# A Mamba-2 block and a selective scan over 16 images: token halves on 128 partitions, step length with B and C, decays one unit ahead

## The chip, the cores and the metric
One NeuronCore of a Trainium2 chip runs one program. The metric is the device time of an execution in microseconds, the median of the runs. Five engines work side by side: TensorE (PE), VectorE (DVE), ScalarE (ACT), GpSimd (POOL) and SyncE (SP), which issues all transfers of this kernel. They are held in step by semaphores, and each runs its own instructions in the order in which they are written.

## The reference
The input has 16 images of 192 channels and 32x32 = 1024 tokens. Two residual blocks follow each other, all in float32:
```python
x = x + L0(group_norm(x))      # Mamba-2 ("SSD"): 384 inner channels, 12 heads of 32, state 32
x = x + L1(group_norm(x))      # selective scan: 192 channels, state 16

# L0, by token
z, xBC, dt = split(u @ in_proj.T)          # 384, 384+32+32, 12
dt = softplus(dt + dt_bias)
x, B, C = split(silu(depthwise_conv3x3(xBC)))
y = chunked_scan(x, dt, -exp(A_log), B, C, chunk=128) + D * x
out = (layer_norm(y) * norm_w + norm_b) * z @ out_proj.T

# L1, by token
x, delta, B, C = split(seq @ W_proj.T + b_proj)   # 192, 192, 16, 16
delta = softplus(delta + dt_bias)
h = exp(delta * A) * h + (delta * x) * B          # (192, 16) states
out = (sum_n(h * C) + x * D) @ W_out.T + b_out
```

## The kernel before, in words
Channels lie on partitions and tokens along the free dimension. 192 channels are 128 and 64, so each image has an "a" tensor on 128 partitions and a "b" tensor (`xb`, `x1b`, `xnb`) on 64, both with 1024 columns.

The passes form a pipeline over images. In pass b the second block's scans of image b run, and between them the whole first block of image b+1, and the last products of image b-1. A pass has 48 slots; on every engine the code of slot s stands ahead of that of slot s+1. Slot by slot:

- **Scans.** The 192x16 states are 24 units of 128 rows (32 channels by 4 states) for each half of 512 tokens, so 48 units. For unit i ScalarE makes the decay exp(delta*A) (`decay`), VectorE the input `wr` and, one slot later, the scan `hst` (`scan_unit`), GpSimd the product with C (`hc`), and TensorE sums the states in batches of two units (`sum_states`). A decay goes to a PSUM bank (units 0 to 7 and 38 to 47: banks 0 and 1; 31 to 35: banks 6 and 7) or to one of three places `dec` in SBUF; `decay_bank` says which. For the first 24 units ScalarE also copies the scan's last column (`carry`), after the slot's other work. `hst` has three places, and scan i waits for the carry of unit i-3.
- **The front of the next image**, slots 0 to 12. VectorE normalises the image (`normalise_groups`), TensorE projects it in nine fills (`fill`: six of 128x512 outputs for x, one for B and C on 64 outputs with both halves in one bank, one for their edge rows, and one with tokens on the partitions for the 12 step lengths, in 8 chunks). ScalarE copies the fills out (`copy_fill`), SyncE makes shifted copies of them with 8 transfers for each piece, and TensorE does the four convolutions (`conv`) at slots 3, 5, 7 and 10. The step lengths go through softplus on ScalarE and VectorE and a cumulative sum on TensorE (`cs_ps`).
- **The chunks**, from slot 13: every second slot starts one of eight chunks of 128 tokens: masked row differences (`rows`), exponentials on ScalarE (`exp_rows`), attention product on VectorE (`attention`), y, layer norm, gate (`gate`), output product (`projected`) and residual (`residual`). A chunk's last stage is 9 slots behind its first, so the last residual is in slot 36.
- **After the chunks**: group statistics (`channel_stats`), a second normalisation at slot 40, the second block's projection in eight pieces (`project`, slots 40 to 46), copies by ScalarE (`copy_projected`) and softplus.
- **The finish of a half** (`finish`): TensorE adds the residual and the output projection into two banks in four steps, one for each slot, and ScalarE copies out in the second and the fourth. Half 0 begins at slot 38 into banks 6 and 7, half 1 at slot 10 of the next pass into banks 0 and 1.

The last pass has scans alone; a pass ahead of the first has only the first image's first block.

## Time and profile before

| | |
|---|---|
| median of 3 runs | 3477.97 us (3474.12 to 3478.38) |
| the profiled execution | 3468.43 us; its span from first to last instruction is 3466.7 us |
| granted TensorE clock, mean | 0.911 of full speed |
| busy: TensorE, VectorE, ScalarE, GpSimd | 2881.6, 2827.0, 1853.7, 1554.3 us |

Busy times are unions of an engine's instructions. A row of a timeline gives the start in microseconds from the span's start, the duration (of a merged run of like instructions, whose number is the x at the end), engine, line, operation, output<-inputs by name (`ssd` holds many tensors of the first block, `bank` is any PSUM bank), shapes, and in brackets the engine's idle time before it with what ended that. A float32 product is two instructions in the records.

### The profile page before, as it was taken

The page shows a single profiled execution, that of the slowest core. Times are in us where ns is not written, and L with a number is a line of the kernel's source. Part 1 is how long each engine was busy: PE and PEld are TensorE (multiplying, and loading weights), DVE is VectorE, ACT ScalarE, POOL GpSimd, SP SyncE. Part 2 cuts the span into 40 slices and gives each one's busy share as a digit, 9 for nine tenths or more (in the row PEclk, how much of TensorE's full clock was granted, in tenths as well). Part 3 has the DMA queues.
Part 4 walks back from the last instruction along what each step waited for, and adds up shares of the span by engine and source line. Part 5 has one row for each costly group of instructions (what it writes and reads, how often), then busy time and mean ns, then how long its engine had stood idle before and what let it go on. Part 6 is the DMA issues. An engine that isn't in the chain of part 4 may idle for free. (4 is left out here: it accounts for less than half of the span.)

```text
span 3466.7 us, 61986 instructions
## 1 busy us (share of the span) xinstructions
PE 2881.6 (83%) x20640; PEld 1535.8 (44%) x20640; DVE 2827.0 (82%) x4364; ACT 1853.7 (53%) x4379; POOL 1554.3 (45%) x1107
## 2 busy tenths in 40 slices
PE   3788888988888888888888888888888988888865
PEld 2554445354443635445354443535445354443510
DVE  1458979798797978979698796978979798897997
ACT  1647474653747456464654746456374654636542
POOL 2115544444444444444344444444444444444455
PEclk8999999998999999999999999989899999989976
DMA  2042141423215142231423214142231424214131
GB/s 58 17 116 71 66 112 53 116 71 109 76 47 149 38 138 71 82 102 46 117 71 115 81 48 137 38 137 71 72 107 53 116 71 122 80 45 132 37 113 58
DMA packets 104168, 291.02 MB, mean 84 GB/s; under 512 B 25373, under 2 KB 27020, under 8 KB 103820
## 3 DMA queue, kind: packets, MB, share of 16 engines
q1 hardware_dynamic: 103820, 286.71, 27.6%
q8 instruction: 179, 2.93, 0.4%
q14 instruction: 169, 1.38, 0.1%
HBM read 181.84 MB, written 39.85 MB: 64 GB/s over the span
## 5 line engine op out<-in xcount | busy, mean ns | idle before, releaser
L749 POOL TENSOR_TENSOR hc<-hst,bcrep 128x512 f32<-128x512 f32 x768 | 1212.5, 1579 | 1291.8 <-DVE hst L1246 1263.3
L1295 PE MATMUL bank<-hc,sel 128*32 128x512 f32 x1536 | 431.6, 644 | 113.0 <-POOL hc L749 109.2
L1233 DVE TENSOR_TENSOR wr<-durep,bcrep 128x512 f32<-128x512 f32 x768 | 520.6, 678 | 2.5 <-DMA bcrep<-bc_rows 2.5
L837 ACT ACTIVATE ssd<-bank,ncs 128x128 f32<-128x128 f32 x1536 | 439.4, 386 | 107.6 <-PE bank L1295 107.1
L1246 DVE TENSOR_TENSOR_SCAN hst<-dec,wr 128x512 f32<-128x512 f32 x256 | 390.8, 1527 | 99.1 <-ACT carry L981 71.2
L940 ACT ACTIVATE bank<-durep,aneg 128x512 f32<-128x512 f32 x368 | 252.6, 690 | 194.1 <-DVE hst L1246 149.8
L1295 PE MATMUL bank<-xna,wt0a 128*128 128x128 f32 (+3 forms) x1088 | 315.7, 395 | 45.1 <-DVE xnb L1046 31.7
L1246 DVE TENSOR_TENSOR_SCAN hst<-bank,carry,wr 128x512 f32<-128x512 f32 x240 | 306.5, 1277 | 14.5 <-ACT bank L940 4.8
L1295 PE MATMUL bank<-ssd,wcv 64*32 64x512 f32 (+1 forms) x6144 | 308.1, 544 | 0.0
L1295 PE MATMUL bank<-xnb,wt0b 128*128 128x128 f32 (+3 forms) x1088 | 302.8, 383 | 0.0
L940 ACT ACTIVATE dec<-durep,aneg 128x512 f32<-128x512 f32 x400 | 291.1, 733 | 7.0 <-DVE hst L1246 4.7
L870 ACT ACTIVATE ssd<-bank,nbc,nwc 128x128 f32<-128x128 f32 x384 | 148.1, 455 | 264.0 <-PE bank L1446 264.0
L1378 PE MATMUL bank<-ident,csum 128*128 128x128 f32 x1536 | 251.7, 289 | 23.0 <-ACT ssd L837 15.0
L1109 DVE TENSOR_TENSOR ssd<-ssd,bank 128x1536 f32<-128x1536 f32 x128 | 223.1, 1743 | 39.6 <-ACT ssd L837 23.9
L1295 PEld LDWEIGHTS bank<-xna,wt0a 128*128 128x128 f32 (+1 forms) x1088 | 189.8, 210 | 143.2 <-issue 106.7
L716 POOL TENSOR_TENSOR lrs<-lve,neghalf 128x1 f32<-128x1 f32 x128 | 95.2, 744 | 327.7 <-DVE lve L1097 327.7
L883 ACT COPY ssd<-bank 128x512 f32<-128x512 f32 x128 | 75.1, 586 | 310.0 <-PE bank L1393 310.0
L1378 PEld LDWEIGHTS bank<-ident,csum 128*128 128x128 f32 x1536 | 182.7, 143 | 126.9 <-issue 82.0
L710 POOL TENSOR_TENSOR ssd<-ssd,wend 128x384 f32<-128x384 f32 x112 | 173.0, 1545 | 125.1 <-ACT ssd L883 124.4
L1295 PE MATMUL bank<-ssd,wo 128*128 128x128 f32 (+1 forms) x1536 | 222.6, 290 | 5.6 <-DVE x1b L1122 5.6
L1295 PEld LDWEIGHTS bank<-xnb,wt0b 128*128 128x128 f32 (+1 forms) x1088 | 186.1, 210 | 71.9 <-issue 71.9
L1295 PE MATMUL bank<-ssd 128*32 128x128 f32 (+1 forms) x3296 | 211.4, 305 | 2.5 <-DVE ssd L1091 1.9
(187 smaller groups left out, 5006.3 us busy)
## 6 DMA issues: line engine op xcount, KB each, us to landing
durep<-scratch SPq DMA_DIRECT2D x192, 512.0 KB, 3.9
bcrep<-bc_rows SPq DMA_DIRECT2D x128, 512.0 KB, 5.1
ssd<-stage SPq DMA_DIRECT2D x384, 140.4 KB, 2.9
ssd<-bcst SPq DMA_DIRECT2D x128, 74.4 KB, 2.6
xa<-in_x_dram SPq DMA_DIRECT2D x16, 512.0 KB, 3.9
scratch<-u SPq DMA_DIRECT2D x32, 256.0 KB, 2.1
scratch<-delta SPq DMA_DIRECT2D x32, 256.0 KB, 2.8
out_dram<-x1a SPq DMA_DIRECT2D x16, 512.0 KB, 4.8
```

What stands on the lines that cost most here:

```text
L710: nc.gpsimd.tensor_tensor(xw[:, c % 2, :].rearrange("p (h d) -> p h d", d=HD), xtok[:, c % 2, 0:DI].rearrange("p (h d) -> p h d", d=HD), b ...
L716: nc.gpsimd.tensor_tensor(lrs[:, c % 2:c % 2 + 1], lve[:, c % 2:c % 2 + 1], neghalf[:, 0:1], ALU.pow).then_inc(lrs_ready.sem, 1)
L749: nc.gpsimd.tensor_tensor(hc[:, i % CRING, :], hst[:, i % HRING, :], bcrep[:, g, 1, :], ALU.mult).then_inc(hc_ready.sem, 1)
L837: ins = nc.scalar.activation(att[:, c % 2, h, :], bank[ROW_BANKS[r]][:, k * Q:(k + 1) * Q], ACT.Exp, bias=ncs[:, c, h:h + 1])
L870: ins = nc.scalar.activation(yzt[:, c % 2, m, :], bank[B_CBT][:, (m + 1) * Q:(m + 2) * Q], ACT.Identity, bias=nbc[:, m:m + 1], scale=nwc[: ...
L883: nc.scalar.copy(xtok[:, c % 2, :], bank[B_XY][:, :]).then_inc(xt_copied.sem, 1)
L940: nc.scalar.activation(decay_of(i), durep[:, j % SLOTS_DU, 0, :], ACT.Exp, scale=aneg1[:, g * NB + k:g * NB + k + 1]).then_inc(decay_ready ...
L1109: nc.vector.tensor_tensor(a, a, bc(bank[B_CBT][:, 0:Q].unsqueeze(1), [P, NH, Q]), ALU.mult).then_inc(att_ready.sem, 1)
L1233: nc.vector.tensor_tensor(wr[:, i % WRING, :], durep[:, j % SLOTS_DU, 1, :], bcrep[:, g, 0, :], ALU.mult).then_inc(w_made.sem, 1)
L1246: nc.vector.tensor_tensor_scan(hst[:, i % HRING, :], decay_of(i), wr[:, i % WRING, :], carry[:, g:g + 1] if hf else 0.0, ALU.mult, ALU.add ...
L1295: return nc.tensor.matmul(out, lhsT, rhs, start=start, stop=stop, skip_group_check=True)
L1378: nc.tensor.matmul(ps[:, k * Q:(k + 1) * Q], bc(csum[:, 0, c, h:h + 1], [P, P]), ident[:, :], start=(k == 0), stop=False, is_transpose=Tru ...
```

## The change
It has five parts.

1. **Halves on 128 partitions.** `xb`, `x1b` and `xnb` become 128x512: tokens 0 to 511 on partitions 0 to 63, tokens 512 to 1023 on 64 to 127. Weights of the "b" products stand twice, on both halves of the partitions; the gate's stand in `wtz`, filled with zeros for the other half. `fill` and `project` handle both halves of a piece together: first product, first product, second product on rows 0 to 63, second product on rows 64 to 127. The biases of the second block's projection, until now rows of the weights against ones in `xnb`, are added by ScalarE in its copies. Statistics take one instruction for the b tensor.
2. **Step length with B and C.** The 12 rows ride along in the B and C fill (76 outputs, a bank for each half; the edge rows are copied from these). VectorE adds the bias out of the banks into `dtt`, TensorE transposes four times (`step_lengths`), ScalarE copies to `dtx`.
3. **Half 0's finish at slot 31** in place of 38. Units 31 to 35 go to `dec`.
4. **Decays one unit ahead.** In slot s ScalarE makes decay s+1 (0 and 1 in slot 0), then the carry of scan s-2, then the slot's other work. Units 0 to 8 take banks 0, 1 and one place of `dec` in turn.
5. **Projection in four pairs** at slots 40 to 43, in the order dA, BC, xA, xdB.

The diff, cut to its core:
```diff
-FILL_AT = (0, 0, 1, 1, 1, 1, 2, 2, 2)
-FILL_COPY_AT = (0, 0, 1, 1, 2, 2, 2, 3, 3)
+FILL_AT = (0, 0, 1, 1, 1, 1, 2, 2)
+FILL_COPY_AT = (0, 0, 1, 1, 2, 2, 3, 3)
...
-P1_AT = (4, 4, 5, 7, 7, 8, 9, 10)
+P1_AT = (4, 5, 6, 7)
...
-END_AT = (38, 10)
+END_AT = (31, 10)
...
-P1_TILES = (("dA", 0), ("BC", 0), ("xA", 0), ("xdB", 0), ("xdB", 1), ("dA", 1), ("xA", 1), ("BC", 1))
-K_BC, K_XA, K_MID, K_D2, K_X2 = 2, 3, 5, 6, 7
+P1_PIECES = ("dA", "BC", "xA", "xdB")
+P1_TILES = [(what, h) for what in P1_PIECES for h in range(2)]
...
+K_D2, K_BC, K_XA, K_X2, K_MID = 2, 3, 5, 6, 8
...
+FRONT_UNITS = 9
...
-    if i < 8 or i >= 38:
+    if i < FRONT_UNITS:
+        return (0, 1, None)[i % 3]
+    if i >= 38:
         return i % 2
-    return 6 + i % 2 if 31 <= i < 36 else None
...
-DECAY_HOME = [i % DRING + 8 if decay_bank(i) is None else decay_bank(i) for i in range(UNITS)]
+    return None
...
+DECAY_HOME = [(8 if i < FRONT_UNITS else i % DRING + 8) if decay_bank(i) is None else decay_bank(i) for i in range(UNITS)]
...
+                if s == 3:
+                    act.wait_ge(dt_ps.sem, dt_ps.at(n, 1))
+                    by_half = bank[B_DT][:, :].rearrange("p (c h k) -> p h c k", c=CPH, h=2)
+                    for h in range(2):
+                        ins = nc.scalar.copy(dtx[:, h * CPH:(h + 1) * CPH, :], by_half[:, 1 - h, :, 0:NH])
+                    ins.then_inc(dtx_ready.sem, 1)
...
-                        decay(b, s, end, first)
+                        for i in (0, 1) if s == 0 else (s + 1,) if s + 1 < UNITS else ():
+                            decay(b, i, end, first)
+                        if 2 <= s < HU + 2:
+                            keep_carry(b, s - 2)
...
-                if s == 3:
...
-                    dve.wait_ge(fill_copied.sem, fill_copied.at(n, 7))
-                    nc.vector.tensor_tensor(dtx[:, :, :], dtx[:, :, :], bc(dtb[:, :].unsqueeze(1), [P, NCH, NH]),
-                                            ALU.add).then_inc(dtx_ready.sem, 1)
+                if s == 2:
...
+                    dve.wait_ge(fill_ps.sem, fill_ps.at(n, 6))
+                    for h in range(2):
+                        nc.vector.tensor_scalar(dtt[(1 - h) * CB_:(1 - h) * CB_ + NH, :], bank[FILL_BANKS[(4 + h) % 3]][2 * NS:2 * NS + NH, :],
+                                                dtb[2 * NS:2 * NS + NH, :], None, ALU.add).then_inc(dtt_ready.sem, 1)
...
+                m, h = FILL_TILES[k]
+                c0, w = DI + m * P, P if m < XM else 2 * NS + NH
+                ps = [bank[FILL_BANKS[(k + h) % 3]] for h in range(2)]
+                for h in range(2):
+                    if k + h >= 3:
+                        pe.wait_ge(fill_copied.sem, fill_copied.at(n, k + h - 2))
+                    if k + h == 7:
+                        pe.wait_ge(dtt_ready.sem, dtt_ready.at(n, 1))
+                    mm(ps[h][0:w, :], wt0a[:, c0:c0 + w], xna[:, h * HALF:(h + 1) * HALF], True, False)
+                for h in range(2):
+                    rows = slice(h * CB_, (h + 1) * CB_)
+                    mm(ps[h][0:w, :], wt0b[rows, m * P:m * P + w], xnb[rows, :], False, True).then_inc(fill_ps.sem, 1)
+
+            def step_lengths(n):
+
+                pe.wait_ge(dtt_ready.sem, dtt_ready.at(n, 2))
+                pe.wait_ge(fill_copied.sem, fill_copied.at(n, 6))
+                for c in range(CPH):
+                    ins = nc.tensor.transpose(bank[B_DT][:, c * P:(c + 1) * P], dtt[:, c * Q:(c + 1) * Q], ident[:, :])
+                ins.then_inc(dt_ps.sem, 1)
...
+                for h in range(2):
+                    mm(outs[h], wt1a[:, c0:c0 + w], xna[:, h * HALF:(h + 1) * HALF], True, False)
+                for h in range(2):
+                    rows = slice(h * CB_, (h + 1) * CB_)
+                    mm(outs[h], wt1b[rows, c0:c0 + w], xnb[rows, :], False, True).then_inc(p1_ps.sem, 1)
```
The last blocks are, in this order, of `first_block` and `run` on ScalarE, of `first_block_soon` on VectorE, and of `fill`, `step_lengths` and `project` on TensorE. `keep_carry(n, i)` waits for scan i and copies its last column; `FILL_TILES` numbers the pieces x0, x0, x1, x1, BC, BC, x2, x2, the halves in turn. At the start three more loads are made, the projection's biases as columns, and a dozen more copies of weights.

## Rows read from the trace of the kernel before
**Rows 1.** Busy time of the engines, the page's first part
```profile
PE 2881.6 (83%) x20640; PEld 1535.8 (44%) x20640; DVE 2827.0 (82%) x4364; ACT 1853.7 (53%) x4379; POOL 1554.3 (45%) x1107
```
**Rows 2.** Windows of one image: length, busy us by engine, granted clock
```profile
1461.00:1530.00 69.00, 62.25 (x549) 26.11 (x546) 47.45 (x55) 50.61 (x103) 29.86 (x20) 0.93 0.49 135
1530.00:1621.00 91.00, 74.49 (x593) 51.15 (x593) 85.18 (x154) 45.81 (x137) 42.41 (x32) 0.94 0.16 56
...
sum 208.00, PE 177.24 PEld 94.35 DVE 176.80 ACT 115.59 POOL 96.57; mean PE 44.31 PEld 23.59 DVE 44.20 ACT 28.90 POOL 24.14
```
**Rows 3.** Timeline of TensorE in that image's front: start, us, instruction, idle before
```profile
1463.66 1.10 PE L1295 MATMUL bank<-xna,wt0a 128*128 128x512 f32 x2 [2.25 <-DVE xnb L1046]
...
1470.70 1.08 PE L1295 MATMUL bank<-xna,wt0a 128*64 128x512 f32 x4
...
1472.82 1.05 PE L1295 MATMUL bank<-hc,sel 128*32 128x512 f32 x4
1473.80 0.39 PE L1295 MATMUL bank<-wt0a,xna 128*128 128x12 f32 x2
...
1477.99 2.06 PE L1295 MATMUL bank<-xna,wt0a 128*128 128x512 f32 x2
...
1484.49 5.38 PE L1295 MATMUL bank<-ssd,wcv 64*32 64x512 f32 x96
...
1515.58 1.12 PE L1295 MATMUL bank<-y1a,wo1a 128*128 128x512 f32 x2
...
1521.80 0.65 PE L1378 MATMUL bank<-ident,csum 128*128 128x128 f32 x4
```
**Rows 4.** Timeline of ScalarE in the same front
```profile
1465.66 0.59 ACT L825 COPY stage<-bank 128x512 f32<-128x512 f32 x1 [1.31 <-PE bank L1295]
...
1525.47 2.17 ACT L837 ACTIVATE ssd<-bank,ncs 128x128 f32<-128x128 f32 x8
```
**Rows 5.** Timeline of VectorE in the same front
```profile
1461.31 1.50 DVE L1045 TENSOR_SCALAR xna<-xa,gm,gr 128x1024 f32<-128x1024 f32 x1 [0.18 <-PE bank L1295]
1462.72 0.80 DVE L1046 TENSOR_SCALAR xnb<-xb,gm,gr 64x1024 f32<-64x1024 f32 x1
...
1496.69 0.36 DVE L1144 COPY csum<-bank 128x192 f32<-128x192 f32 x1 [5.67 <-PE bank L1295]
...
1503.54 1.22 DVE L1246 TENSOR_TENSOR_SCAN hst<-bank,wr 128x512 f32<-128x512 f32 x1 [0.50 <-ACT carry L981]
...
1529.42 1.74 DVE L1109 TENSOR_TENSOR ssd<-ssd,bank 128x1536 f32<-128x1536 f32 x1
```
**Rows 6.** Timeline of VectorE in the last pass
```profile
3413.89 2.11 DVE L1246 TENSOR_TENSOR_SCAN hst<-dec,carry,wr 128x512 f32<-128x512 f32 x1
...
3416.68 1.28 DVE L1246 TENSOR_TENSOR_SCAN hst<-bank,carry,wr 128x512 f32<-128x512 f32 x1
...
3418.63 1.28 DVE L1246 TENSOR_TENSOR_SCAN hst<-bank,carry,wr 128x512 f32<-128x512 f32 x1
```
**Rows 7.** Groups of VectorE by line and form: busy us, mean ns, idle before
```profile
L1025 DVE BATCH_NORM_STATS2 st<-x1b 64x6 f32<-64x512 f32 x32 | 21.4, 668 | 0.0
...
L1045 DVE TENSOR_SCALAR xna<-xa,gm,gr 128x1024 f32<-128x1024 f32 x16 | 19.4, 1211 | 21.7 <-issue 12.2 <-PE bank L1295 8.6 <-POOL gr L701 0.9
```
**Rows 8.** Timeline of all engines around a first block's last gate
```profile
1832.75 0.55 PE L1446 MATMUL bank<-ident,ssd 128*128 128x128 f32 x3 [2.34 <-DVE ssd L1101]
...
1834.79 0.54 DVE L1115 TENSOR_TENSOR ssd<-ssd,bank 128x384 f32<-128x384 f32 x1
```
**Rows 9.** Timelines of VectorE and ScalarE around one chunk's exponentials
```profile
1776.57 1.21 DVE L1246 TENSOR_TENSOR_SCAN hst<-dec,wr 128x512 f32<-128x512 f32 x1
...
1777.29 0.72 ACT L940 ACTIVATE dec<-durep,aneg 128x512 f32<-128x512 f32 x1
1777.91 1.13 ACT L837 ACTIVATE ssd<-bank,ncs 128x128 f32<-128x128 f32 x4
1779.91 1.16 ACT L870 ACTIVATE ssd<-bank,nbc,nwc 128x128 f32<-128x128 f32 x3 [0.86 <-PE bank L1446]
```

## What the change will do, predicted from these rows

> **What bounds the kernel now.** I read the page first: VectorE is busy for 2827.0 us and TensorE for 2881.6 us of a span of 3466.7 us [rows 1]; neither share says which one sets the end. So I cut one image out of the middle, from VectorE's normalisation of one image to that of the next, and asked for the windows [rows 2]: 208 us, in which VectorE works 176.8 us. The reader is to see that its idle 31 us are not spread. In the first 69 us (slots 0 to 14, where the next image's projections and convolutions are made) it works 47.5 us and TensorE 62.3; in the next 91 us (the chunks of the first block) VectorE works 85.2. So an image is a front of some 69 us that TensorE's chain sets, and then some 139 us that VectorE sets. The timelines show what closes each wait. TensorE starts the fills at 1463.66 and the first convolution only at 1484.49, 20.8 us later [rows 3]. VectorE, always early, waits for what comes behind them: for the cumulative sum (5.67 us before 1496.69), for ScalarE's carry before the scan at 1503.54, and it starts the first attention product at 1529.42 [rows 5], 68.1 us after the image's start.
>
> **The front, part by part.** (a) The eight chunks of step lengths cost TensorE the stretch from 1473.80 to 1477.99, 4.2 us; they go. What replaces them are 12 rows more in the B and C products, which cost nothing by themselves, and four transposes, 0.6 us by the group of four 128x128 transposes at 1521.80. (b) Each 512-column product on 128 rows takes two instructions; eight of them fill the time from 1463.66 to 1470.70 [rows 3], 0.88 us each, and I count 0.86, twice 0.43. In the new order two first products come, then two second ones on rows 0 to 63 and 64 to 127 into two banks. Do these two overlap? No such pair is in the trace. The nearest row is the convolution: 96 instructions of 512 columns on 64 rows by 32 columns in 5.38 us [rows 3]; one at 0.43 us after another would need 41 us, so 7.6 run at once, and four column places alone would give 4. Rows 0 to 63 and 64 to 127 are thus worked at the same time there. I take full overlap, 0.86 us less for each of three pairs: 2.6 us; the bound from below is nothing.
> The Trainium skill, "TensorEngine Tiling (Array Packing)", section Tiling Modes, lists 64x128 as two independent tiles of the array; by it a pair costs one product, as in my sum, and without it rival Two holds. The same section lists 128x64 as two tiles, which the old B and C product of 64 columns uses and the new one of 76 can't: that speaks against this part.
> (c) That loss by rows: the old B and C products with their edge rows took 2.1 us (1470.70 to 1472.82, where a batch sum begins); the new ones take two first products and an overlapped pair, 3 x 0.86 = 2.6: 0.5 us more. (d) The second tensor's normalisation, 0.80 us on 1024 elements [rows 5], has half the elements: 0.4 us earlier. (e) Against it: TensorE now finishes a piece faster than ScalarE empties banks. ScalarE's first copy is at 1465.66 [rows 4], and three softplus activations of the last projection, 0.6 to 0.7 us each like other activations of 512 columns [rows 9], stand between the second and third; the second decay now stands ahead of the first copy as well and waits for the previous image's last scan. From the image's start: last scan done at 3.1 us, decay 3.8, three activations 5.7, first copy 6.3, where TensorE wants its fourth first product at 5.4: 0.9 us late, of which the order of the banks hides 0.1; in the same way the copy that the sixth waits for comes at 9.9 and not 8.9. So 1.8 us back. VectorE's two additions of 512 columns out of the banks (0.6 us each, as the statistics on 512 columns [rows 7]) replace one of 96; they stand in a stretch where it waits. Sum for the chain: 4.2 + 2.6 + 0.4 - 0.6 - 0.5 - 1.8 = 4.3 us.
> (f) Decays one unit ahead. The scan at 1503.54 waited 0.50 us for ScalarE's carry, which stood behind the convolution's copies; it now stands ahead: 0.5 us. At the end of the front ScalarE finished the exponentials of chunk 0 at 1527.64 [rows 4], but VectorE came to the attention product at 1529.42, since its scans had waited for decays behind the copies: 1.8 us. New ones go ahead, so 1.8 us. What is late next: units 8 and 9 share one place, so ScalarE waits for scan 8 ahead of the third convolution's copies, and VectorE gets its scans 10 to 14 one behind the other; by the step of 2.79 us for each [rows 6] it arrives just when the exponentials are there. Front in all: 4.3 + 0.5 + 1.8 = **6.6 us** an image.
>
> **The rest of the image.** (g) Statistics: the four pieces of 64 rows become two of 128, so two instructions of 0.67 us, 0.6 when they overlap, go [rows 7]: 1.2 us, in stretches where VectorE never waits. The second normalisation gives 0.4. VectorE's wait ahead of the first normalisation (21.7 us in 16 images, a part of it ahead of the first scan; I take 1.1 us an image [rows 7]) goes, as the projections end three slots sooner; but VectorE's product of the first piece needs xA, now one slot later and behind a decay and a copy after scan 42: 0.7 us of waiting. Net 0.4. (h) Units 31 to 35 leave the banks for SBUF. The last pass, which has nothing but scans, prices that: from a scan with its decay in SBUF to the next start 2.79 us, with it in a bank 1.95 [rows 6]: 0.84 us when GpSimd's product runs beside it. Units 34 and 35 follow closely, the other three lie behind other work: 1.7 us (bounds 0 and 4.2). (i) The finish at 31. TensorE now has half 0's late products (about 1.05 us each, the row at 1515.58) straight behind the last transposition of y at 1832.75, and ScalarE waits for them in slot 32, ahead of the scaling that VectorE's last gate needs. Before: transposition, scaling, gate at 1834.79 [rows 8]. After: transposition to 1833.2, two products 2.1, ScalarE's output 0.7 and one decay 0.7 as in [rows 9], the scaling 1.1, gate at about 1837.9: **3.1 us** later, and VectorE has nothing else to do there (bounds 0, if the products get in ahead, and 5.5 at half the clock). The old place cost nothing: ScalarE waited there, VectorE did not.
> An image: -6.6 - 1.2 - 0.4 - 0.4 + 1.7 + 3.1 = **-3.8 us**. Fifteen passes have a front: -57. The last pass has only scans; seven units more read from SBUF: 7 x 0.84 = +6. Ahead of the first scan I count nothing: the first image's front gives about 4 us, and three more loads and a dozen more weight copies, an estimate of mine without a row, take it back. In all -51 us against the profiled execution's 3468.4 us. The runs' median is 3478.0, 9.5 us above that execution; I take the same difference from it: **3427 us**.
>
> **The rivals.**
> One, the finish is hidden (chance 0.17): TensorE gets the late products done before the transposition is ready, and the 3.1 us vanish. For it: it idles 2.34 us ahead of 1832.75. Against: the order on the engine is fixed, the transposition stands first. -6.9 an image: 3478 - 104 + 6 = 3380.
> Two, the pairs don't overlap (0.20): each second product runs alone; 2.6 us are lost, and the B and C pair another 0.9, but the 1.8 us of waiting for copies goes with it. -2.1 an image: 3478 - 31 + 6 = 3453.
> Three, it ends slower: ScalarE is held to one unit (0.15). In the chunks, decay s+1 waits for scan s-2 where decay s waited for scan s-3. The exponentials at 1777.91 began 0.14 us after the end of scan 21 at 1777.78; the decay (0.7 us) and the carry (0.1) now come between. I count nothing, because ScalarE idles 0.86 us ahead of its scaling at 1779.91 [rows 9]. If that idle time isn't there, all eight chunks pay 0.8 us: +6.4, so +2.6 an image, 3478 + 39 + 6 = 3523. It decides from 0.45 us a chunk.
> Four, no change (0.12): VectorE's additions at slot 2 stand behind the sixth fill, the scan behind them, GpSimd's product behind the scan and TensorE's batch sum behind that; if this chain closes the front, it gains 3.2 and not 6.6 us, and the last pass takes the rest: 3478.
> My forecast has 0.36, with 3405 to 3448 as its own range.
>
> **How the numbers follow.** Two kernels are told apart here from about 0.2%, 7 us. Faster: forecast, One, Two, 0.36 + 0.17 + 0.20 = 0.73; same 0.10, slower 0.17 from Three and the upper half of Four. The range reaches from below One to just above Four, 3370 to 3486; it leaves out Three and little else.
>
> **What would show it.** Right: the start of the first convolution some 4 us nearer to the normalisation; no idle VectorE ahead of the seventh and eleventh scans; the second products on 64 rows as overlapping pairs; scans on SBUF at 2.1 us in units 34 and 35; VectorE idle 3 us ahead of its last gate. Wrong: exponentials in the chunks that start 0.8 us later against the scan; pairs 0.86 us apart; a granted clock in the front far from the 0.93 of now [rows 2], which would move the chain by more than any of these terms.

## The result, and the profile after

The changed kernel takes 3429.8 us (median of 4 runs, 3427.84 to 3430.25) against 3476.05 for the kernel before (4 runs, 3473.64 to 3478.38): ratio 0.9866, 95% interval 0.9849 to 0.9883. The forecast was 3427. The profiled executions differ by 40.6 us (3468.4 to 3427.84).

Busy times on the page after, to be read beside [rows 1]:
```profile
PE 2789.6 (81%) x20064; PEld 1392.5 (41%) x20064; DVE 2839.9 (83%) x4350; ACT 1905.2 (56%) x4425; POOL 1555.6 (45%) x1108
```
TensorE has lost 92 us of work, VectorE has gained 13, and the time went down by 41: shares say no more than that. The window of one image's front, cut as the first in [rows 2]:
```profile
1449.00:1515.00 66.00, 57.97 (x505) 20.31 (x502) 48.76 (x56) 51.13 (x104) 30.61 (x20) 0.89 0.54 148
```
The front is 3 us shorter at a lower granted clock (0.89, before 0.93). TensorE's timeline in that front, against [rows 3]:
```profile
1451.65 3.75 PE L1336 MATMUL bank<-xna,wt0a 128*128 128x512 f32 x4 [1.13 <-DVE xnb L1088]
1455.34 2.02 PE L1336 MATMUL bank<-xnb,wt0b 64*128 64x512 f32 x4
1457.29 1.98 PE L1336 MATMUL bank<-xna,wt0a 128*128 128x512 f32 x4
1459.20 1.13 PE L1336 MATMUL bank<-xnb,wt0b 64*128 64x512 f32 x4
1460.26 2.27 PE L1336 MATMUL bank<-xna,wt0a 128*76 128x512 f32 x4
1462.47 1.08 PE L1336 MATMUL bank<-xnb,wt0b 64*76 64x512 f32 x4
1463.48 1.05 PE L1336 MATMUL bank<-hc,sel 128*32 128x512 f32 x4
1464.46 1.98 PE L1336 MATMUL bank<-xna,wt0a 128*128 128x512 f32 x4
1466.38 1.13 PE L1336 MATMUL bank<-xnb,wt0b 64*128 64x512 f32 x4
1467.44 0.66 PE L1375 MATMUL bank<-ident,dtt 128*128 128x128 f32 x4
1467.93 0.28 PE L1336 MATMUL bank<-ident 128*128 128x1 f32 x2
1468.14 5.38 PE L1336 MATMUL bank<-ssd,wcv 64*32 64x512 f32 x96
...
1490.85 1.51 PE L1336 MATMUL bank<-hc,sel 128*32 128x512 f32 x4 [4.18 <-POOL hc L772]
...
1494.52 5.44 PE L1336 MATMUL bank<-ssd,wcv 64*32 64x512 f32 x96
...
1506.11 0.65 PE L1416 MATMUL bank<-ident,csum 128*128 128x128 f32 x4
...
1510.59 0.65 PE L1416 MATMUL bank<-ident,csum 128*128 128x128 f32 x4 [2.04 <-ACT ssd L865]
```
From the first fill to the first convolution it is 16.5 us, before 20.8. Four instructions on 64 rows (a pair of second products) take 1.06 us from start to start, four on 128 rows 1.92: the pairs overlap. ScalarE and VectorE in the same front:
```profile
1491.91 0.72 ACT L974 ACTIVATE dec<-durep,aneg 128x512 f32<-128x512 f32 x1 [3.67 <-DVE hst L1287]
...
1492.73 1.28 ACT L825 ACT_TABLE_LOAD   x1
...
1509.39 1.14 ACT L865 ACTIVATE ssd<-bank,ncs 128x128 f32<-128x128 f32 x4
```
```profile
1463.63 1.52 DVE L1177 TENSOR_SCALAR dtt<-bank,dtb 12x512 f32<-12x512 f32 x2 [4.76 <-PE bank L1336]
...
1498.97 1.22 DVE L1287 TENSOR_TENSOR_SCAN hst<-dec,wr 128x512 f32<-128x512 f32 x1 [3.72 <-ACT carry L980]
...
1514.82 1.75 DVE L1150 TENSOR_TENSOR ssd<-ssd,bank 128x1536 f32<-128x1536 f32 x1 [3.77 <-PE bank L1336]
```
VectorE no longer waits for the cumulative sum (5.67 us ahead of scan 5 in [rows 5]). It waits 4.8 us for the B and C fill, out of whose banks it now adds the step lengths' bias, 3.7 us ahead of scan 10, for a carry that stands behind the third convolution's copies, and 3.8 ahead of the first attention product.

Around the last gate, TensorE, ScalarE and VectorE, against [rows 8]:
```profile
1604.31 0.55 PE L1484 MATMUL bank<-ident,ssd 128*128 128x128 f32 x3 [1.02 <-DVE ssd L1142]
1604.69 1.02 PE L1336 MATMUL bank<-y1a,wo1a 128*128 128x512 f32 x2
1605.64 1.12 PE L1336 MATMUL bank<-y1b,wo1b 64*128 64x512 f32 x2
```
```profile
1606.81 0.69 ACT L999 ACTIVATE x1a<-bank,boc 128x512 f32<-128x512 f32 x1 [8.54 <-PE bank L1336]
1607.39 0.71 ACT L974 ACTIVATE dec<-durep,aneg 128x512 f32<-128x512 f32 x1
1608.00 1.15 ACT L904 ACTIVATE ssd<-bank,nbc,nwc 128x128 f32<-128x128 f32 x3
```
```profile
1609.18 0.55 DVE L1156 TENSOR_TENSOR ssd<-ssd,bank 128x384 f32<-128x384 f32 x1 [2.51 <-ACT ssd L904]
```
From the transposition to the gate it is 4.9 us, before 2.0. The finish stands between.

To see where the time went over the whole run I took the starts of all 768 scans from each trace; a row of this table is the mean of the 15 passes with a front, in us from the scan that opens the stretch to the one that opens the next. Under "run", ratio to the kernel before in the timed runs:

```
slots            0-1   2-9  10-15 16-18 19-26 27-31    32    33 34-35 36-40 41-43 44-47    sum  run
before         14.61 32.49  22.76 19.06 43.13 24.16  2.88  2.18  5.80 16.34 12.01 11.06 206.46
after          16.33 28.47  21.28 17.23 43.13 23.34  5.93  2.42  7.28 15.31 11.94 10.63 203.29  0.9866
serial         28.89 33.07  21.43 18.76 43.16 23.75  5.16  2.42  7.28 15.38 26.14 10.27 235.69  1.1366
wide           17.37 28.47  21.04 18.02 43.15 23.47  5.64  2.42  7.28 15.36 11.95 10.64 204.82  0.9950
same_rows      18.46 28.46  21.69 18.44 43.13 23.58  5.63  2.42  7.28 15.38 17.68 10.18 212.32  1.0264
noahead        16.16 25.83  22.74 18.82 43.15 23.67  5.27  2.42  7.39 15.39 11.86 10.59 203.28  0.9898
fin38          16.06 28.56  21.28 16.91 43.14 23.20  3.01  2.56  7.28 15.41 17.10 10.30 204.81  0.9945
fin32          16.29 28.63  21.29 17.11 43.16 23.28  3.83  2.42  7.28 15.27 11.67 10.69 200.90  0.9784
front8         16.03 24.92  23.39 17.76 43.15 24.00  4.84  2.42  7.28 15.28 12.32 10.70 202.10  0.9838
both           16.14 24.90  23.35 17.12 43.13 23.56  2.77  2.68  7.28 15.15 11.77 10.77 198.60  0.9678
conv9b         15.73 24.93  21.64 17.74 43.13 23.20  2.89  2.52  7.28 15.15 12.05 10.68 196.92  0.9609
end14          16.04 24.92  22.17 18.11 43.13 23.77  2.59  2.67  7.29 15.16 12.07 10.69 198.62  0.9691
warm           15.53 24.92  21.05 18.31 43.12 23.60  2.72  2.67  7.29 15.14 11.66 10.86 196.88  0.9603
best_old_order 16.64 25.81  21.92 18.04 43.13 23.67  2.71  2.65  8.10 15.16 11.68 10.90 200.40  0.9768
```

After less before: 3.17 us an image, 47.6 in 15 passes; the last pass is 5.9 us longer and the first scan 1.1 later, which makes the 40.6. The front (slots 0 to 15) gives 3.78 and slots 16 to 18 another 1.83; slot 32 takes 3.05 back, slots 34 and 35 take 1.48. The chunks of slots 19 to 26 are the same to 0.01 us. One of the four runs of same_rows took 3608.5 us, over 1.5% more than its fastest: its ratio leaves that run out, its median below counts it.

The means hide one thing, which matters for every comparison below. Slots 16 to 18 take 16.8 to 16.9 us in each image in which TensorE has full clock there, and 18.3 to 19.9 in each in which the granted clock is at half for a part of them, and that holds for the kernel before, the changed one and all edits but end14 (there 17.8, and 18.3 to 19.4). Of the 15 images, those with full clock in slots 16 to 18 are 1 before, 12 in the changed kernel, none in serial, 1 in noahead and in same_rows, 6 in wide, 13 in fin32 and in the run named both, 15 in fin38, 7 in front8, conv9b and best_old_order, 4 in warm, 11 in end14 (under 1 us at half clock counts as none). So the 1.83 us there are the clock's. The same 24 instructions of TensorE in slot 17 of one image, first in noahead, at half clock, and then in the changed kernel:
```profile
1528.61 1.51 PE L1335 MATMUL bank<-ssd 128*32 128x128 f32 x24
```
```profile
1528.30 0.86 PE L1336 MATMUL bank<-ssd 128*32 128x128 f32 x24
```

### The profile page after: what moved, and what is told of

Its sections match the earlier page's. It is cut to its first block and busy times, and to the rows that moved or that the text cites. A ratio compares the mean times of both kernels' runs of the same rounds, so it can differ in the third digit from the quotient of the medians.

```text
span 3426.1 us, 60703 instructions
## 1 busy us (share of the span) xinstructions
PE 2789.6 (81%) x20064; PEld 1392.5 (41%) x20064; DVE 2839.9 (83%) x4350; ACT 1905.2 (56%) x4425; POOL 1555.6 (45%) x1108
## 3 DMA queue, kind: packets, MB, share of 16 engines
q14 instruction: 165, 1.35, 0.1%
## 5 line engine op out<-in xcount | busy, mean ns | idle before, releaser
L772 POOL TENSOR_TENSOR hc<-hst,bcrep 128x512 f32<-128x512 f32 x768 | 1193.3, 1555 | 1179.9 <-DVE hst L1287 1150.2
L1336 PE MATMUL bank<-hc,sel 128*32 128x512 f32 x1536 | 467.0, 691 | 196.1 <-POOL hc L772 170.4
L974 ACT ACTIVATE dec<-durep,aneg 128x512 f32<-128x512 f32 x512 | 369.0, 725 | 329.5 <-DVE hst L1287 316.2
L1287 DVE TENSOR_TENSOR_SCAN hst<-dec,wr 128x512 f32<-128x512 f32 x288 | 419.1, 1455 | 84.9 <-ACT carry L980 72.8
L974 ACT ACTIVATE bank<-durep,aneg 128x512 f32<-128x512 f32 x256 | 175.4, 689 | 378.6 <-DVE hst L1287 332.1
L1336 PE MATMUL bank<-xna,wt0a 128*128 128x128 f32 (+2 forms) x1024 | 314.1, 399 | 24.7 <-DVE xnb L1088 21.5
L1287 DVE TENSOR_TENSOR_SCAN hst<-dec,carry,wr 128x512 f32<-128x512 f32 x224 | 315.5, 1409 | 5.0
L1336 PEld LDWEIGHTS bank<-xna,wt0a 128*128 128x128 f32 (+1 forms) x1024 | 175.9, 204 | 173.4 <-issue 101.6
L1336 PEld LDWEIGHTS bank<-hc,sel 128*32 128x32 f32 x1536 | 58.2, 113 | 408.0 <-POOL hc L772 274.7
L1287 DVE TENSOR_TENSOR_SCAN hst<-bank,carry,wr 128x512 f32<-128x512 f32 x160 | 204.7, 1280 | 8.5
```

The lines of the kernel that those rows point to most:

```text
L772: nc.gpsimd.tensor_tensor(hc[:, i % CRING, :], hst[:, i % HRING, :], bcrep[:, g, 1, :], ALU.mult).then_inc(hc_ready.sem, 1)
L974: nc.scalar.activation(decay_of(i), durep[:, j % SLOTS_DU, 0, :], ACT.Exp, scale=aneg1[:, g * NB + k:g * NB + k + 1]).then_inc(decay_ready ...
L1287: nc.vector.tensor_tensor_scan(hst[:, i % HRING, :], decay_of(i), wr[:, i % WRING, :], carry[:, g:g + 1] if hf else 0.0, ALU.mult, ALU.add ...
L1336: return nc.tensor.matmul(out, lhsT, rhs, start=start, stop=stop, skip_group_check=True)
```

## The experiments

Each is an edit of the changed kernel or of the best one so far, timed beside the kernel before on the same chip, whose median lay between 3469 and 3472 us there. I compare ratios.

**Where the finish of half 0 stands: fin32 and fin38.**
```
-END_AT = (31, 10)
+END_AT = (32, 10)     # fin32;  fin38: (38, 10)
```


> Half 0's finish one slot later (32 in place of 31), nothing else. My theory (the price of the new finish is ScalarE's output copy standing ahead of the scaling that VectorE's last gate needs; in the changed kernel VectorE idles 3.0 us there in each image): with the copy one slot later it stands behind the scaling, the wait goes, and nothing else becomes late: 2.8 us an image over 15 images, 42 us less, 3388 us. Rival (the late products delay TensorE's own work, the gate products and the output projection, wherever they stand): the wait moves from the gate to the residual one or two slots on, and the time stays within 10 us of the changed kernel's 3430.

> Half 0's finish put back to 38, where the kernel before had it; units 31 to 35 still take their decays from SBUF. My theory: at 38 ScalarE's wait for the late products has nothing of VectorE's behind it, so the 2.8 us an image go as with 32: 3388 us. Rival (the finish at 38 now meets the projections at 40 to 43, which end three slots sooner than before, and the pair of banks that they share): VectorE's first normalisation of the next image, or its product of the first piece, waits 1 to 3 us more, and 3400 to 3430 us come out.

fin32: 3392.9 us, ratio 0.9784 (0.9748 to 0.9821), 0.8% below the changed kernel's. Slot 32 gives 2.1 us back: ScalarE's copy, with the two late products that it waits for, was most of the price. The two moved together, so their shares are not told apart. What was kept is 1.5 us of waiting for TensorE, which makes the finish's first identity product ahead of the last gate's product. fin38: 3452.6 us, 0.9945 (0.9929 to 0.9962), 0.8% slower than the changed kernel: my theory missed. Slot 32 gives 2.9 back, slots 41 to 43 take 5.2. TensorE, ScalarE and VectorE of that kernel:
```profile
1630.03 2.06 PE L1336 MATMUL bank<-x1a,ident 128*128 128x512 f32 x2
1632.14 2.08 PE L1336 MATMUL bank<-y1a,wo1a 128*128 128x512 f32 x2
...
1638.00 2.43 PE L1336 MATMUL bank<-xna,wt1a 128*128 128x512 f32 x4
```
```profile
1641.68 1.27 ACT L943 ACTIVATE delta<-bank,p1b 128x512 f32<-128x512 f32 x2 [3.33 <-PE bank L1336]
```
```profile
1644.82 0.43 DVE L1092 TENSOR_SCALAR u<-ssd 128x512 f32<-128x512 f32 x1 [2.66 <-ACT ssd L953]
...
1651.23 0.69 DVE L1252 TENSOR_TENSOR u<-delta,xcm 128x512 f32<-128x512 f32 x1 [2.02 <-ACT xcm L943]
```
The finish's products (6.1 us here, at half clock) stand ahead of the projections, which now come at slots 40 to 43 and for which ScalarE and then VectorE wait. So the earlier finish is not a loss of 3.1 us on its own: it keeps its products out of the way of the projections, and it was one or two slots too early.

**Do the pairs pay? serial, same_rows and wide.** serial orders the products of both blocks first, second, first, second:
```
 for h in range(2):
     mm(ps[h][0:w, :], wt0a[:, c0:c0 + w], xna[:, h * HALF:(h + 1) * HALF], True, False)
-for h in range(2):
     rows = slice(h * CB_, (h + 1) * CB_)
     mm(ps[h][0:w, :], wt0b[rows, m * P:m * P + w], xnb[rows, :], False, True)
```


> Projections of both blocks in the order first product, second product, first product, second product, so that no second product on rows 0 to 63 has one on rows 64 to 127 beside it; banks, waits and operands unchanged. My theory (pairs overlap, and TensorE's products close the front): four pairs in the front fall apart at 0.86 us each, the first convolution starts 3.4 us later and so does the attention; 52 us more, 3482 us. Rival (the pairs overlap, but ScalarE or a scan closes the front): under 1 us an image, below 3445 us. Were the pairs not overlapping at all, the time would not move.

3945.8 us, 1.1366 (1.1347 to 1.1385): 516 us more than the changed kernel, ten times the 52 of my theory, and the rival had none. The granted clock is 0.50 from 1455 to 1475 (third number from the end of the window) and the mean over the run 0.824 (changed kernel 0.904). The window, and TensorE's timeline:
```profile
1455.00:1475.00 20.00, 17.49 (x18) 4.32 (x18) 8.81 (x10) 8.71 (x15) 5.43 (x4) 0.50 0.62 187
```
```profile
1457.51 2.07 PE L1336 MATMUL bank<-xna,wt0a 128*128 128x512 f32 x2 [3.18 <-DVE xnb L1088]
1459.51 2.07 PE L1336 MATMUL bank<-xnb,wt0b 64*128 64x512 f32 x2
...
1483.05 2.08 PE L1336 MATMUL bank<-xna,wt0a 128*128 128x512 f32 x2
1485.06 1.23 PE L1336 MATMUL bank<-xnb,wt0b 64*128 64x512 f32 x2
```
Every product takes 1.9 to 2.0 us, full or half of the rows, until 1485; in [rows 3] the same order took 0.88 each (the old second products ran on 128 rows, half of them zeros). So I asked whether it is the rows. same_rows keeps the order of the changed kernel and lets both second products of a pair use the same rows. It leaves out the second half's own rows, so its output is not the reference's, and its times serve for comparison alone:
```
-rows = slice(h * CB_, (h + 1) * CB_)
+rows = slice(0, CB_)
```


> The changed kernel with its order of products kept (two first ones, two second ones), but both second products of a pair take the weights and the data of rows 0 to 63, so the second half's projections are computed from the first half's second rows. The order that drew TensorE down to half its clock in the last set is not in it. My theory (pairs overlap, and each of four pairs in the front is worth 0.86 us at full clock, 1.7 at half, where the first one stands): the attention starts 3.4 to 4.3 us later, 3480 to 3495 us. Rival one (the two products of a pair can't be told apart by rows and do not overlap): 3425 to 3435 us. Rival two (the clock again: without the overlap TensorE stays at half clock through the fills): over 12 us an image, above 3600 us.

3572.7 us, 1.0264 (1.022 to 1.0309), 4% above the changed kernel: between my theory and rival two, with a mean granted clock of 0.887. The first convolution starts 20.9 us from the normalisation (mean of 11 images) and not 18.5, the attention only 1.3 us later and not 3.4; but slots 41 to 43, where the second block is projected, take 5.7 us more. And wide is serial with all 128 rows in the first block's second products:
```
-mm(ps[h][0:w, :], wt0b[rows, m * P:m * P + w], xnb[rows, :], False, True)
+mm(ps[h][0:w, :], wt0b[:, h, m * P:m * P + w], xnb[:, :], False, True)   # zeros on the other half's rows
```


> The changed kernel with the first block's second products on all 128 rows, each with weights that are zero on the other half's 64 rows, in the order first, second, first, second. Against the run with that order on 64 rows only the rows differ; the result is the reference's. The projections of the second block stay in pairs. Theory one (TensorE fell to half its clock there because half of its rows stood idle in every second product): the fills run at full clock, but for those that start them; the first convolution starts about 3.4 us later than in the changed kernel, and the attention 2 to 4; 3455 to 3490 us. Theory two (the order, or the products without a partner, brings the half clock, whatever the rows): the first convolution starts over 10 us later, 3600 us and more.

3452.0 us, 0.9950 (0.9935 to 0.9966), 0.8% above the changed kernel. TensorE of wide:
```profile
1460.50 2.05 PE L1337 MATMUL bank<-xna,wt0a 128*128 128x512 f32 x2 [1.14 <-DVE xnb L1089]
1462.34 1.92 PE L1337 MATMUL bank<-xnb,wt0b 128*128 128x512 f32 x2
1464.05 1.91 PE L1337 MATMUL bank<-xna,wt0a 128*128 128x512 f32 x2
1465.76 1.24 PE L1337 MATMUL bank<-xnb,wt0b 128*128 128x512 f32 x2
1466.83 1.02 PE L1337 MATMUL bank<-xna,wt0a 128*128 128x512 f32 x2
```
Theory one holds: with the order of serial and full rows the clock is back at full after three products. One other thing differs between the two kernels, the order of the second block's projections. It does not reach into these fills: in serial those projections end at full clock (1.00 from 1440 to 1450), and the clock falls only in the idle time ahead of the fills, as it does in wide. The size was less than I had expected: the first block's pairs are worth 1.35 us of the first convolution's start (19.8 us from the normalisation against 18.5) and 1.5 us an image in the table, of which 0.8 stand in slots 0 to 15 and 0.8 in slots 16 to 18, where the clock fell in 9 images and not in 3. What the second block's pairs are worth was not measured by itself.

**The lead of the decays: noahead.**
```
-for i in (0, 1) if s == 0 else (s + 1,) if s + 1 < UNITS else ():
-    decay(b, i, end, first)
-if 2 <= s < HU + 2:
-    keep_carry(b, s - 2)       # now behind first_block, as before
+decay(b, s, end, first)
```


> The changed kernel with ScalarE's decays and carries in their old order: decay s in slot s, the carry behind the slot's copies. All else as changed. The prediction's term (f) says 2.3 us an image lost: 3464 us. My theory after the traces: no more than 0.7 us an image either way, 3420 to 3440 us, since in the changed kernel the exponentials of chunk 0 stand behind two decays more and VectorE waits 3.4 us for them; without the lead they start 1.5 us earlier and VectorE comes 1.8 us behind them.

3435.0 us, 0.9898 (0.9879 to 0.9918), inside my range and far from the 3464 of term (f); the interval overlaps the changed kernel's, and the profiled span is the same (3426.4 against 3426.1). In the changed kernel the lead costs the front 1.35 us (slots 0 to 15). The 1.6 that it saves in slots 16 to 18 are the clock's: without the lead it falls there in 14 images of 15, with it in 3.

**Unit 8: front8, both and conv9b.**
```
-FRONT_UNITS = 9
+FRONT_UNITS = 8                 # front8
+END_AT = (33, 10)               # both: with front8
+CONV_AT = (3, 5, 7, 9)          # conv9b: with both; was (3, 5, 7, 10)
```


> Unit 8 leaves the first SBUF place, so units 8 and 9 no longer share one; nothing else. ScalarE then does not wait for scan 8 ahead of the third convolution's copies, and VectorE's idle 3.7 us ahead of scan 10 should go. Theory one (that wait lies on the path of the front): 3.7 us an image, 3375 us. Theory two (the front is closed by TensorE's fourth convolution and the exponentials behind it, and VectorE was only early): the same time, 3425 to 3435 us, with the 3.7 us back as a longer wait ahead of the first attention product, 3.4 us now and about 7 then. I hold theory two for the likelier.

> Half 0's finish at 33, and unit 8 out of the place that unit 9 takes. At 33 the first product of the finish (2.1 us) stands behind the last chunk's gate product and not ahead of it: the 1.5 us that VectorE still waited for TensorE with the finish at 32 become 0.7. Against the changed kernel: 2.2 + 0.7 us an image for the finish, 0.9 for the place; 3.8 by 15 = 57 us less, 3372 us. Rival (the later output meets the projections, as at 38, where VectorE lost 7 us an image around them): the gain of the finish shrinks below that of 32, 3385 to 3400 us.

> The kernel of the run before (finish at 33, unit 8 moved) with the fourth convolution in slot 9 in place of 10. In the changed kernel TensorE idles 4.2 us ahead of it, in front of a batch sum that waits for scan 7, and scan 7 waits for the logarithm behind ScalarE's copies. In slot 9 it stands ahead of that sum. My theory: the fourth convolution starts up to 4.2 us earlier, and the front ends 2 to 4 us earlier: 3310 to 3340 us. Rival one (the data of the fourth convolution is not there, or its bank not yet copied): the wait stays, same time as the run before. Rival two (ScalarE's third and fourth copies now close the front): under 1 us an image.

front8: 3412.8 us, 0.9838 (0.9821 to 0.9854). Slots 2 to 9 lose 3.6 us of waiting, slots 10 to 15 take 2.1 back, 16 to 31 another 1.2, and slot 32 gives 1.1; nearer to theory two, but with 1.2 us an image left over where I had said none. What slots 16 to 31 take goes with the clock too: it is at half somewhere in slots 27 to 31 in all 15 images (24.0 us), in the changed kernel in 6 (22.9 where it is not). The wait did not come back at the attention, as I had thought (3.4 to 3.0 us), but one convolution later, ahead of scan 13 (0.8 us at scan 13 before, now 2.7). both: 3360.6 us, 0.9678 (0.9662 to 0.9694), better than my 3372; slot 32 is at 2.77, under that of the kernel before. conv9b: 3336.3 us, 0.9609 (0.9592 to 0.9626). TensorE of conv9b around the fourth convolution:
```profile
1448.06 1.05 PE L1336 MATMUL bank<-hc,sel 128*32 128x512 f32 x4
1450.43 0.38 PE L1336 MATMUL bank<-ident 128*128 128x1 f32 x2 [1.32 <-DMA ssd<-stage]
1450.74 5.38 PE L1336 MATMUL bank<-ssd,wcv 64*32 64x512 f32 x96
```
It starts 6.6 us earlier (37.9 us from the normalisation, in both 44.5), held by its shifted copies now; but the rows start only 4.7 earlier and the attention 2.4, because ScalarE's copies and VectorE's scans come next. The gain is 1.7 us an image, just under the 2 to 4 that I had expected; the time lies inside my range.

**The other finish: end14.**
```
-END_AT = (33, 10)
+END_AT = (33, 14)
```


> The kernel with finish at 33, unit 8 moved and the fourth convolution in slot 9 (3336 us), and with it half 1's finish of the previous image in slots 14 to 17 in place of 10 to 13. TensorE has 8.4 us between the end of the fourth convolution and the first rows of the attention, 4.2 of them the late products of that finish and 1 its last identity product; ScalarE has its two output copies ahead of the exponentials. My theory: the exponentials start 4 to 6 us earlier, VectorE then has its scans 13 to 15 to do and takes 2 us of that: 1.9 us an image, 3300 to 3315 us. Rival (the late products now delay TensorE's transpositions and outputs of chunk 0, for which VectorE waits 0.8 and 1.0 us already): the gain is given back there, 3330 to 3345 us.

3360.3 us, 0.9691 (0.9661 to 0.9721), 0.8% slower than conv9b: worse than the rival. The rows start 2.1 us earlier, the exponentials 1.2 and the attention 0.5 later; slots 16 to 18 and 27 to 31 take 0.9. As I read it, the late products at slots 10 to 13 mostly filled time in which TensorE waits for ScalarE's copies ahead of the rows. The clock fits that reading: with them gone it is at half for a part of slots 10 to 15 in all 15 images, for 6.8 us in the mean where it was 3.2 in conv9b. Which part of the loss is the clock's and which is the products' new place was not tested.

**The clock: warm.**
```
+def warm(times):
+    for _ in range(times):
+        mm(bank[3][:, :].rearrange("p (b c) -> p b c", c=BLK), ident[:, :], wcv[:, 0:P // 8, :], True, True)
```


> The kernel with finish at 33, unit 8 moved and the fourth convolution in slot 9 (3336 us), and in it products that compute nothing used (constants by 512 columns, into a bank that is free): three in slot 46, one ahead of the wait for the normalised image, two in slot 38 and one ahead of the wait for the second normalised image. They stand where TensorE idles (2.9 and 1.1 us ahead of the fills, 1.8 and 1.0 ahead of the second block's projections) and change no wait. In the kernel without them the granted clock is 0.5 from 5.8 or 7.5 us ahead of an image's first scan for 7 to 10 us, and the first products take 0.9 us an instruction pair's half in place of 0.5. My theory: the clock falls because TensorE idles there, and stays up with them; the first fills take 1.5 to 2.6 us less and the first projections 1.8, of which VectorE sees 1.3: 2.8 to 3.9 us an image, 3278 to 3294 us. Rival one (the clock falls at that place whatever TensorE does): 3336 to 3345 us, the products only in the way. Rival two (the clock stays up here and falls elsewhere instead): the same time within 10 us, with the drop at another slot.

3330.9 us, 0.9603 (0.9574 to 0.9632), not to be told from conv9b, with a mean granted clock of 0.941 against 0.914. TensorE of warm:
```profile
1411.79 2.84 PE L1336 MATMUL bank<-wcv,ident 128*128 128x512 f32 x6 [0.67 <-ACT delta L936]
...
1415.55 1.13 PE L1336 MATMUL bank<-wcv,ident 128*128 128x512 f32 x2
1416.96 1.98 PE L1336 MATMUL bank<-xna,wt0a 128*128 128x512 f32 x4 [0.28 <-DVE xnb L1088]
...
1421.52 1.13 PE L1336 MATMUL bank<-xna,wt0a 128*128 128x512 f32 x2 [0.47 <-ACT stage L853]
```
In this image the clock stays up. The fills take 1.2 us less from their first to the first convolution (14.2 against 15.4 us), but start 0.8 later, and ScalarE's copies, which the half clock had hidden, now hold TensorE. The front (slots 0 to 15) gains 0.8 us, and slots 16 to 31 take back 1.0. The clock stayed up at the fills as my theory had it, and the time stayed as rival two had it, for two reasons. One is that rival's own: the time at half clock went from 5.4 to 1.6 us an image in slots 0 to 15, and from 4.4 to 7.4 in slots 16 to 31, which is where the 1.0 us went. The other is not in it: where the clock stayed up, ScalarE's copies stood right behind it.

**The lead again, on the best kernel: best_old_order** (the edit of noahead on conv9b).

> The kernel with finish at 33, unit 8 moved and the fourth convolution in slot 9 (3336 us), with decay s back in slot s and the carry behind the copies. On the changed kernel this return of the old order took 1.35 us off the front (slots 0 to 15) and put 1.6 on slots 16 to 18, 0.3 on 27 to 31 and took 0.7 off slot 32, in the profile nothing altogether, in the timed runs 0.3% slower with overlapping intervals. Theory (the lead of the decays is worth nothing in the front and saves about 1.6 us in chunk 0 alone): here too the front is about 1 us an image shorter and the next slots 1.5 longer, and since the finish no longer holds slot 32, its 0.7 does not come back: 0.5 to 1.2 us an image slower, 3343 to 3356 us. The prediction's term (f), 2.3 us an image lost: 3370 us. Rival (the exponentials of chunk 0 close the front, and the lead delays them): 3315 to 3330 us, faster.

3390.9 us, 0.9768 (0.9752 to 0.9784), 1.7% slower than conv9b and slower than all three expectations; the 3370 of term (f) comes nearest. The lead is worth nothing in the changed kernel and 3.5 us an image here: 2.1 in slots 0 to 15, 0.8 in slots 27 to 31 and 16 to 18, 0.8 in slots 34 and 35, where scan 35 now waits for its decay. As I read it, the shared place of units 8 and 9 and the early finish had hidden it in the changed kernel. That is not shown: these two and the fourth convolution's slot are what differs, and they were not put back one at a time.

## Why the prediction came out

The time was right (3429.8 against 3427), the account only in part, and that the two times lie so near is partly luck. By its own steps the gain was 51 us; the profiled executions show 40.6, the medians 46.2. The largest difference is in the front.

- **(a) step lengths**: right. 4.19 us went, 0.49 came (predicted 4.2 and 0.6). This is read from the timelines; no run puts the old step lengths back.
- **(b) pairs**: right in kind, mis-sized. A set of four products takes 2.98 us (1464.46 to 1467.44) where it took 3.52 in [rows 3]: 0.54 and not 0.86, because two first products one after the other take 1.92 and not 1.72, and a pair 1.06. Three sets 1.6, predicted 2.6. The table of tilings that the Trainium skill gives ("TensorEngine Tiling (Array Packing)", section Tiling Modes) puts 64x128 down as two independent tiles: the trace agrees, four 64-row instructions in 1.06 us. It also lists 128x64 as two tiles, and there the rows agree as well: the four old B and C products of 64 columns took 2.12 us with their edge rows (1470.70 to 1472.82 in [rows 3]), four of 128 columns 3.52.
- **(c) B and C**: mis-sized. 3.22 us (1460.26 to 1463.48) for 2.12: 1.1 and not 0.5.
- **(d), (e)**: the earlier normalisation does not show in that image (2.36 us from its start to the first fill, before 2.35). The waits for ScalarE's copies, 1.8 us in the sum, are 0.3 (the 2.27 at 1460.26 for 1.98). What took their place is the granted clock: the first pair of the front runs at half, 5.64 us for a set of 2.98. The old front lost as much on its last set (6.29 for 3.52), so the clock left the sum as it was, and moved. As warm shows, at full clock the copies do hold TensorE.
  Together: the first convolution 4.3 us nearer in that image (5.6 in the mean of 11), predicted 4.3. The terms missed in both directions.
- **(f) decays ahead**: this is the step that failed. "It arrives just when the exponentials are there" was said of VectorE alone. The exponentials themselves came 1.7 us later behind the fourth convolution (9.3 us for 7.6), with more decays and carries ahead of them on ScalarE (noahead takes 1.2 of it back), and the fourth convolution gained 0.85 us less than the first, behind scan 7. So the front gave 3.8 us and not 6.6. A sign that I had named failed with it: VectorE idles 3.7 us ahead of the eleventh scan, scan 10, where it was not to idle. Slots 16 to 18 gave 1.8 us where I had counted nothing: the clock, for which the sum has no term. That units 8 and 9 share a place was seen and priced at nothing; it cost 1.2 us an image (front8).
- **(g)**: right. Slots 27 and 40 are 0.6 us shorter each. The wait ahead of the first normalisation did not vanish (21.7 us in 16 images before, 13.8 now), and slots 41 and 42 are no shorter: 0.5 us net over slots 41 to 47, predicted 0.8.
- **(h)**: right. Slots 34 and 35 take 1.5 us more, predicted 1.7; the last pass 5.9, predicted 6. VectorE in the last pass:
```profile
3388.65 2.11 DVE L1287 TENSOR_TENSOR_SCAN hst<-dec,carry,wr 128x512 f32<-128x512 f32 x1
...
3391.44 1.28 DVE L1287 TENSOR_TENSOR_SCAN hst<-bank,carry,wr 128x512 f32<-128x512 f32 x1
```
- **(i)**: right in place and size, 3.05 us in slot 32, predicted 3.1. From the transposition to the gate it is 2.8 more. "The old place cost nothing" was true of the old kernel and false of the new one (fin38).
- **Rivals.** One: slot 32 refutes it. Two: refuted by wide, though half of it was true, since the pairs give less than I took. Three: its sign came (at scan 21 the exponentials start 0.75 us behind the scan's end, before 0.14, in the mean of 14 images), its cost did not: slots 19 to 26 are the same to 0.01 us, as ScalarE's idle time took it up. Four is nearest to what failed: something behind the fills closes the front, but as far as the runs show it was ScalarE at its end and not the sum at slot 2.

The front's 2.8 us too many stood against 1.8 in slots 16 to 18, which the clock gave and I had not seen. What was left, some 10 us, was covered by the base, and that is the luck in the figure: the profiled execution of before was 8 us faster than its median (3468.4 against 3476.05), that of after only 2 (3427.84 against 3429.8). A right time is weak evidence for its terms; the table by slots is what tested them.

What stays open: why the clock falls in slots 16 to 18 of some images and not of others; why the timed runs of noahead lie 0.3% above the changed kernel's where the profiles are equal; and the 0.25 us more in each of slots 29, 31 and 33, whose scans take no longer.

## What to carry to other kernels

Cut a pipelined kernel by a marker that every image has (here the scans) and compare two versions stretch by stretch: the gain, what gives it back and where then stand in one table. When work moves earlier on one engine, follow the queue of the engine that serves it to the first thing that another engine waits for; here a finish begun one or two slots too early cost 2.4 us an image (fin32 against the changed kernel) to 3.5 (both against front8), the same reordering was worth nothing or 3.5 us depending on three constants around it, and these three (finish 33, unit 8, fourth convolution at 9) took the kernel from 0.9866 to 0.9609. Before a stretch's gain is put down to the change, look at the granted clock in it, image by image: slots 16 to 18 took 16.9 us or 18.3 and more in one and the same kernel. And a move that looks like a plain loss may be what another part stands on: test it by undoing it before calling it one.

## What the hardware showed that I had not expected

- How soon TensorE's granted clock came back went with the rows that its instructions use. It was at half ahead of the fills in wide and in serial. The same sequence of products ran at full clock from the fourth one on with 128 rows each (wide), and stayed at half (2.0 us a product for 0.86) for 28 us with 64 rows in every second one, though TensorE worked without a gap (serial). Once the clock was up, the products on 64 rows did not bring it down in the rows seen (1.00 from 1440 to 1450 in serial). With both blocks' products in that order the kernel took 15% longer than the changed one.
- In the changed kernel the clock fell to 0.50 while TensorE idled for 2.9 us ahead of the fills (the windows below, the granted clock again third from the end), and the first set of products ran at it. Products that compute nothing used, put into such gaps, raised the mean clock from 0.914 to 0.941, and the time did not follow.
```profile
1446.00:1448.00 2.00, 0.00 (x0) 0.00 (x0) 1.91 (x3) 1.65 (x3) 1.67 (x2) 0.73 0.94 320
1448.00:1450.00 2.00, 1.41 (x4) 0.19 (x4) 2.00 (x3) 0.69 (x1) 1.59 (x2) 0.50 0.66 246
```
- Two products on rows 0 to 63 and 64 to 127 take 1.06 us together at full clock, where one on all rows takes 0.86 to 0.88 (wide, [rows 3]).
